# Local attention on array tiles: 64x32 for the scores, 64x64 for P times V

## The reference

```
for layer in range(6):
    h = shift_tokens(x)                      # half of the channels from the token before
    q, k, v = split(h @ Wqkv[layer], 3)      # 16 heads x 64 each
    q, k = l2norm(q) * q_scale, l2norm(k) * k_scale, then rotary tables
    # windows of 32 queries; each sees the keys of its own window and of the one before
    sim = einsum('bhwie,bhwje->bhwij', q, [k_before, k_own]) * 8.0     # 32 x 64 per window
    sim = where(j < i or j > i + 32 or no such key, -max, sim)
    out = einsum('bhwij,bhwje->bhwie', softmax(sim), [v_before, v_own])
    x = out @ Wo[layer] + x
    x = (a * gelu(gate)) @ W2 + b2 + x,   with a, gate = layernorm(shift_tokens(x)) @ W1 + b1
```

## Time and the profile before

| | |
|---|---|
| median of 3 runs | 1647.47 us (1647.35 to 1647.62) |
| profiled execution, its own time | 1648.04 us |
| its span | 1646.3 us |
| PE busy | 1580.4 us (96%) |
| VectorE busy | 1421.3 us (86%) |
| GpSimd busy | 1369.4 us (83%) |
| ScalarE busy | 1331.9 us (81%) |

### The profile page before, as it was taken

One profiled execution on the slowest core, in us unless ns is written; L12 is line 12 of the kernel. 1 busy time (PEld: TensorE's weight loads), 2 busy tenths in 40 slices (PEclk: granted clock), 3 DMA queues, 4 the chain that ended last, 5 costly groups with the idle time before them and its releaser, 6 DMA issues.

```text
span 1646.3 us, 51246 instructions
## 1 busy us (share of the span) xinstructions
PE 1580.4 (96%) x20015; PEld 1345.6 (82%) x20015; DVE 1421.3 (86%) x2163; ACT 1331.9 (81%) x2516; POOL 1369.4 (83%) x1323
## 2 busy tenths in 40 slices
PE   5999999999999999999999999999999999999976
PEld 3778888888888888888888888888888888888865
DVE  7888888989888888888888888889888899999964
ACT  5778788888888888888888888888888888888862
POOL 8888899888899888889888889988889777777632
PEclk9999999999999999999999999999999999999998
DMA  5334222433332334333343232334323222322231
GB/s 146 96 85 130 74 86 76 119 113 89 98 94 67 107 101 115 83 90 91 84 124 103 82 99 73 104 87 129 96 72 101 66 78 71 88 76 66 64 85 28
DMA packets 182430, 149.64 MB, mean 91 GB/s; under 512 B 133804, under 2 KB 153904, under 8 KB 182192
## 3 DMA queue, kind: packets, MB, share of 16 engines
q1 hardware_dynamic: 182192, 146.35, 31.7%
HBM read 27.56 MB, written 1.05 MB: 17 GB/s over the span
## 4 chain that ended last, share of the span: by engine, by line
PE 67%; DVE 12%; issue 6%; ACT 5%; POOL 4%; SPq 2%; DMA 2%; ACTq 0%; DVEq 0%; POOLq 0%
PE ps_pv L851 10%; PE ps_s L827 8%; PE ps_pv L872 7%; PE ps_tr L788 7%; PE ps_qn L763 7%; PE ps_qn L765 5%; PE ps_qn L764 5%; PE ps_tr L775 4%; PE ps_pv L863 3%; DVE ss L1513 3%; DVE v_new L1524 2%; PE ps_qn L910 2%; POOL qk L1967 2%; PE ps_qn L911 2%; PE ps_qn L912 2%
## 5 line engine op out<-in xcount | busy, mean ns | idle before, releaser
L1967 POOL TENSOR_TENSOR qk<-qk,t 128x1024 f32<-128x1024 f32 x192 | 458.9, 2392 | 42.2 <-DVE qk L1503 40.8
L1500 DVE TENSOR_TENSOR t<-ps_qn,tab 128x512 f32<-128x512 f32 x384 | 264.9, 690 | 119.6 <-ACT sq L1150 109.6
L1979 POOL TENSOR_TENSOR qkr<-qk,rinv 128x1024 f32<-128x1024 f32 x192 | 361.5, 1904 | 7.5
L763 PE MATMUL ps_qn<-w_hi,xs_hi 128*128 128x512 f32 x576 | 262.7, 456 | 10.7 <-DVE qk L1503 7.4
L1137 ACT ACTIVATE pbd<-ps_tr 64x512 f32<-64x512 f32 x384 | 226.0, 589 | 45.7 <-PE ps_tr L775 42.5
L1503 DVE TENSOR_TENSOR qk<-ps_qn,tab 128x512 f32<-128x512 f32 x384 | 261.6, 681 | 0.0
L1150 ACT ACTIVATE sq<-ps_qn 128x512 f32<-128x512 f32 x384 | 229.2, 597 | 32.1 <-PE ps_qn L765 27.3
L1182 ACT ACTIVATE qbd<-ps_tr 64x512 f32<-64x512 f32 x384 | 227.9, 593 | 18.9 <-PE ps_tr L788 12.5
L764 PE MATMUL ps_qn<-w_lo,xs_hi 128*128 128x512 f32 x576 | 228.5, 397 | 0.0
L765 PE MATMUL ps_qn<-w_hi,xs_lo 128*128 128x512 f32 x576 | 228.5, 397 | 0.0
L1513 DVE TENSOR_REDUCE ss<-sq 128x32 f32<-128x2048 f32 x96 | 216.7, 2257 | 0.2 <-issue 0.2
(11 more groups left out here) (173 smaller groups left out, 3247.3 us busy)
## 6 DMA issues: line engine op xcount, KB each, us to landing
v_own<-v_new SPq DMA_DIRECT2D x96, 512.0 KB, 3.2
v_back<-v_new SPq DMA_DIRECT2D x96, 384.0 KB, 3.5
v_back<-v_own SPq DMA_DIRECT2D x94, 128.0 KB, 2.4
kT<-kT SPq DMA_DIRECT2D x84, 128.0 KB, 3.4
w_raw<-in_Wqkv SPq DMA_DIRECT2D x18, 512.0 KB, 4.9
rot<-in_rot SPq DMA_DIRECT2D x48, 128.0 KB, 2.6
wo<-in_Wo SPq DMA_DIRECT2D x6, 512.0 KB, 4.5
x<-x SPq DMA_DIRECT2D x48, 56.0 KB
```

The costliest lines, as they stand in the source:

```text
L763: mm(ps_qn[bank][:, :], xs_hi[b][:, :], w_hi[:, part], start=True, stop=False)
L1500: v.tensor_tensor(t2[:, part].rearrange("p (h s d) -> p h s d", s=2, d=DH // 2), swapped, tab[:, 2 * k + 1:2 * k + 2, :].rearrange("p o (s ...
L1967: g.tensor_tensor(qk[b][:, part], qk[b][:, part], t2[:, part], ALU.add).then_inc(added[b], 1)
L1979: g.tensor_tensor(qkr[b][:, part].rearrange("p (h d) -> p h d", d=DH), qk[b][:, part].rearrange("p (h d) -> p h d", d=DH), rinv[b][:, k * ...
```

## The change

Scores and P times V use smaller array tiles whose stationary operands are plain.

- **Scores**: the queries go to `qT` as they are transposed (128 rows x 8 head pairs x 128 tokens). Each matmul holds 32 queries of one head (64 rows x 32 columns) and moves 64 keys; 64 matmuls a half, on eight array tiles (2 row halves x 4 column quarters). `ps_s` is laid out by row half: one bank for each.
- **P times V**: the probabilities go to `pT`, 64 keys on the rows of each half. Each matmul holds 64 keys x 64 columns of the values of a head and moves 32 query columns; 64 matmuls a half, on four array tiles. The two banks of `ps_pv` now belong to the two row halves, and both are full only at the end of f=1.
- **Values**: instead of `v_own` and `v_back` there is `v_win`, for each window its 64 keys on 64 rows, the even heads' on the lower half and the odd heads' on the upper. `move_v` makes it with ten DMAs where there were three.
- **Mask**: two matmuls of 128 rows, no longer of 64.
- **ScalarE**: `evac_probs` and `evac_q` copy 128 rows at once, no longer twice 64.
- **Start and end**: two memsets on GpSimd are gone; in the last steps `scale_probs` of the last half is moved ahead of `low_fxn` and `last_root` there.
- The host permutes columns of `Wqkv` and rows of `Wo` for the new order.

```diff
+V_CARRY, V_MOVE = 2 * 16, 8 * 16
...
-    w.v_own = per_stream("v_own", [P, INNER])
-    w.v_back = per_stream("v_back", [P, INNER])
-    w.qbd = sb("qbd", [P, HP, 4, 2, WINDOW])
+    w.v_win = per_stream("v_win", [P, WINDOWS, HP * DH])
+    w.qT = sb("qT", [P, HP, P])
...
-    w.pbd = sb("pbd", [P, HP, 2, 2, 2, WINDOW])
+    w.pT = sb("pT", [P, HP, P])
...
-        def pv_target(bank, m, h):
-            return ps_pv[bank][DH * h:DH * (h + 1), :].rearrange("p (m u a q) -> p m u a q", m=4, u=2, a=2)[:, m // 2, :, m % 2, :]
+        def pv_rows(bank):
+            return ps_pv[bank][:, :].rearrange("p (g t) -> p g t", g=HP // 2)
...
                 def move_v(i, b):
...
-                    if j.first:
-                        values = a["no_keys"].rearrange("(r k) h w -> r (k h w)", r=WINDOW)
-                    else:
-                        wait_fill(sp, pv_full, pv_order, i, ("pv", b, 1))
-                        values = v_own[b][P - WINDOW:P, :]
-                    sp.dma_start(v_back[b][0:WINDOW, :], values).then_inc(v_carried[b], 16)
+                    def window(h, w, first, last):
+                        return v_win[b][DH * h + first:DH * h + last, w, :]
+
+                    def tokens(h, first, last):
+                        return v_new[b][first:last, h * HP * DH:(h + 1) * HP * DH]
+
+                    if not j.first:
+                        for h in range(2):
+                            wait_fill(sp, pv_full, pv_order, i, ("pv", b, h))
+                    for h in range(2):
+                        if j.first:
+                            values = a["no_keys"].rearrange("(r k) h w -> r (k h w)", r=WINDOW)[:, h * HP * DH:(h + 1) * HP * DH]
+                        else:
+                            values = window(h, WINDOWS - 1, WINDOW, 2 * WINDOW)
+                        sp.dma_start(window(h, 0, 0, WINDOW), values).then_inc(v_carried[b], 16)
                     wait_fill(sp, qn_done, qn_order, j, ("qkv", b, 5))
-                    sp.dma_start(v_back[b][WINDOW:P, :], v_new[b][0:P - WINDOW, :]).then_inc(v_moved[b], 16)
-                    sp.wait_ge(v_carried[b], (j.n + 1) * 16)
-                    sp.dma_start(v_own[b][:, :], v_new[b][:, :]).then_inc(v_moved[b], 16)
+                    for h in range(2):
+                        sp.dma_start(window(h, 0, WINDOW, 2 * WINDOW), tokens(h, 0, WINDOW)).then_inc(v_moved[b], 16)
+                        for w in (1, 2):
+                            sp.dma_start(window(h, w, 0, 2 * WINDOW), tokens(h, WINDOW * (w - 1), WINDOW * (w + 1))).then_inc(v_moved[b], 16)
+                    sp.wait_ge(v_carried[b], (j.n + 1) * V_CARRY)
+                    for h in range(2):
+                        sp.dma_start(window(h, 3, 0, 2 * WINDOW), tokens(h, 2 * WINDOW, P)).then_inc(v_moved[b], 16)
...
                 def mask(i, b):
...
-                    for f in range(2):
-                        rows = slice(64 * f, 64 * f + 64)
-                        mm(ps_s[:, 4 * f:4 * f + 4, :, :].rearrange("p m u k -> p m (u k)"), sel_bf[rows, :],
-                           mask_bf[rows, min(j.tile, 1):min(j.tile, 1) + 1, :].broadcast_to([64, 4, P]), start=True, stop=False)
+                    kind = min(j.tile, 1)
+                    for h in range(2):
+                        mm(ps_s[:, h, :, :].rearrange("p m k -> p (m k)"), sel_bf[:, :],
+                           mask_bf[:, kind:kind + 1, :].broadcast_to([P, HP, 2 * WINDOW]), start=True, stop=False)
...
                 def scores(i, b, f):
...
                     for hp in range(4 * f, 4 * f + 4):
-                        for u in range(2):
-                            for odd in range(2):
-                                w = 2 * u + odd
-                                last = mm(ps_s[64 * odd:64 * odd + 64, hp, u, :],
-                                          qbd[:, hp, w, :, :].rearrange("p h q -> p (h q)"),
-                                          kT[b][:, hp, WINDOW * w:WINDOW * (w + 2)], start=False,
-                                          stop=(hp % 4 == 3 and u == 1))
+                        for h in range(2):
+                            rows = slice(DH * h, DH * (h + 1))
+                            for w in range(WINDOWS):
+                                q = slice(WINDOW * w, WINDOW * (w + 1))
+                                last = mm(ps_s[q, h, hp, :], qT[rows, hp, q], kT[b][rows, hp, WINDOW * w:WINDOW * (w + 2)],
+                                          start=False, stop=hp == HP - 1)
...
                 def probs_v(i, b, f):
...
-                    bank, n = fill(pv_order, i, ("pv", b, f))
-                    ring_free(pe, pv_done, bank, n)
-                    for m in range(8):
-                        hp, odd = 4 * f + m // 2, m % 2
-                        v = (v_own if odd else v_back)[b]
-                        for h in range(2):
-                            head = 2 * hp + h
-                            last = mm(pv_target(bank, m, h), v[:, head * DH:(head + 1) * DH],
-                                      pbd[:, hp, odd, h, :, :].rearrange("p u q -> p (u q)"), start=True, stop=True)
-                    last.then_inc(pv_full[bank], 1)
+                    fills = [fill(pv_order, i, ("pv", b, h)) for h in range(2)]
+                    if f == 0:
+                        for bank, n in fills:
+                            ring_free(pe, pv_done, bank, n)
+                    for g in (2 * f, 2 * f + 1):
+                        for h, (bank, _) in enumerate(fills):
+                            rows = slice(DH * h, DH * (h + 1))
+                            for w in range(WINDOWS):
+                                q = slice(WINDOW * w, WINDOW * (w + 1))
+                                for c in range(2):
+                                    hp = 2 * g + c
+                                    last = mm(pv_rows(bank)[DH * c:DH * (c + 1), g, q], v_win[b][rows, w, hp * DH:(hp + 1) * DH],
+                                              pT[rows, hp, q], start=True, stop=True)
+                            if g == HP // 2 - 1:
+                                last.then_inc(pv_full[bank], 1)
...
-                    wait_fill(act, pv_full, pv_order, pi, ("pv", pb, k))
+                    for h in range(2):
+                        wait_fill(act, pv_full, pv_order, pi, ("pv", pb, h))
                     bank, n = fill(tr_order, i, ("probs", b, k))
                     act.wait_ge(tr_full[bank], n)
-                    for u in range(2):
-                        rows = slice(DH * u, DH * (u + 1))
-                        last = f(pbd[rows, 4 * k:4 * k + 4, :, :, u, :].rearrange("p m a h q -> p (m a h) q"),
-                                 ps_tr[bank][rows, :].rearrange("p (x q) -> p x q", q=WINDOW), ACT.Copy)
-                    last.then_inc(tr_done[bank], 1)
+                    f(pT[:, 4 * k:4 * k + 4, :].rearrange("p m t -> p (m t)"), ps_tr[bank][:, :], ACT.Copy).then_inc(tr_done[bank], 1)
...
-                    for h in range(2):
-                        rows = slice(DH * h, DH * (h + 1))
-                        last = f(qbd[rows, 4 * k:4 * k + 4, :, h, :],
-                                 ps_tr[bank][rows, :].rearrange("p (m w q) -> p m w q", m=4, w=4), ACT.Copy)
-                    last.then_inc(tr_done[bank], 1)
+                    f(qT[:, 4 * k:4 * k + 4, :].rearrange("p m t -> p (m t)"), ps_tr[bank][:, :], ACT.Copy).then_inc(tr_done[bank], 1)
...
-                    g.memset(qbd[:, :, :, :, :], 0.0)
-                    g.memset(pbd[:, :, :, :, :, :], 0.0)
...
                     scale_probs(Step(0, STEPS - 2), 1)
                     scale_probs(Step(0, STEPS - 1), 0)
+                    scale_probs(Step(0, STEPS - 1), 1)
                     low_fxn(END + 1)
                     last_root(END + 1)
-                    scale_probs(Step(0, STEPS - 1), 1)
```

More of the change, by code:

```diff
@@ L26 @@
 HP = HEADS // 2
+WINDOWS = P // WINDOW
 FF = int(DIM * 4 * 2 / 3)
@@ L870, in project_out @@
                         wait_fill(pe, pv_done, pv_order, i, ("pv", b, f))
-                    for hp in range(HP):
-                        last = mm(ps_pv[bank][:, 0:P], oT[:, hp, :, :, :].rearrange("p u a q -> p (u a q)"), wo[:, hp, :],
-                                  start=(hp == 0), stop=(hp == HP - 1))
+                    for n in range(HP):
+                        last = mm(ps_pv[bank][:, 0:P], oT[:, n // 2, n % 2, :], wo[:, n, :], start=(n == 0), stop=(n == HP - 1))
                     return last
@@ L2196, in mask_constants @@
 def mask_constants():
-    m = np.full((2, 2, WINDOW, 2, 2, 2 * WINDOW), MASKED, np.float32)
+    m = np.full((WINDOWS, WINDOW, 2, 2 * WINDOW), MASKED, np.float32)
     q = np.arange(WINDOW)[:, None]
@@ L2202, in mask_constants @@
     ok = (k >= q) & (k <= q + WINDOW)
[L2203 to L2212 removed]
+    for w in range(WINDOWS):
+        for kind in range(2):
+            seen = ok & ((k >= WINDOW) if (w, kind) == (0, 0) else True)
```

(2 more changed lines are left out.)

49 lines of the change are left out of this document (21 added, 28 removed).

## The result

The changed kernel takes 1800.06 us (median of 4 runs, 1786.21 to 1816.87) against 1647.41 for the kernel before (4 runs). The slowest of the four counts as slow and stays out of the ratio, which is 1.090 with a 95% interval of 1.081 to 1.099; the median of the other three is 1790.78. The change cost 152 us by the medians of all runs, and 143 by the median of the three. The forecast was 1672, 25 us slower, so that the loss was about six times the forecast one and the time far outside of the range of 1628 to 1706. The sign was right and the size was not.

What follows compares the result with a forecast made beforehand. PE, busy 96%, was taken as full but in balance with a loop through VectorE and ScalarE. From 1648.0, value moves +33 −4 +3, drain −6 and start −1 gave 1673, or 1672 against the median; range 1628 to 1706.

Steps and rivals of the forecast that it cites:

- The loop, and PE's saved work as no gain: VectorE's less_max, PE's mask and burst two, squares, back to less_max: PE's saved 0.8 us bring 0 in b=0, −0.35 in b=1.
- I take 0.62 from start to start: SyncE's queue: the ten value transfers of a half are issued 0.62 us apart, whatever their size.
- 8.0 us: First value carry to last landing: 9×0.62=5.6 plus 2.4; evac_v in b=0 then misses 1.1, taken as +33 over 33 halves.
- In b=1 ... −0.1 for 37 halves: VectorE's evac_v in b=1: 0.4 us missing, less 0.35 of the loop and lateness of b=0, so −4 in all.
- I take 1.08 unchanged: A burst of P times V on PE: 64 passes on four tiles, 16 each, still take 1.08 us.
- rival B: PE's tiles don't overlap across row halves: a burst of P times V 2.16, scores 2.0, whole 1870 us; chance 0.04.
- Scores 1.0 us: Scores on PE: 128 passes on eight tiles, 16 on each, take 1.0 us, −1.0 us a half.
- C: PE passes can't follow closer than 31.5 and 34 ns on any tiles: scores 4.0, burst 2.2, whole 2060 us; chance 0.03.
- Mask 0.5, and squares later behind both evacuations: PE's mask of two 128-row products takes about 0.5, +0.2; both evac_pv wait for burst two, so squares start +0.3 later.
- ScalarE at nothing: ScalarE's evacuations of probabilities and queries take 2.4 us less a half, costed at nothing in the total.
- Drain −6: End of the kernel: earlier scale_probs on GpSimd saves 4.2 us and fewer copies about 2, together −6.
- Start −1: Before the first tile's scores: the queries' copies shrink from 2.42 to 1.2 us, taken as −1.

Runs made afterwards that it cites:

- three_moves_wide_pv: Changed kernel with three value transfers instead of ten and P times V back on 128x64 stationary pieces (output wrong): 1640.20 us, ratio 0.995 to the kernel before.
- before_ten_moves: Kernel before with only its three value transfers a half split into ten of the same bytes: 1715.23 us, ratio 1.040.
- wide_scores_interleaved_pv: Changed kernel with three value transfers, scores on 128x64 pieces and row halves innermost in P times V (output wrong): 1659.46 us, ratio 1.007 to the kernel before.
- before_drain: Kernel before with only the last half's scale_probs moved ahead of low_fxn and last_root on GpSimd: 1643.34 us, ratio 0.996.
- tile_scores: Kernel before with plain queries in qT and scores in 64 matmuls on 64x32 tiles, in the old layout of the scores: 1660.72 us, ratio 1.008.
- after_three_moves: Changed kernel with three value transfers a half instead of ten, same bytes, values in wrong places: 1717.08 us, ratio 1.042 to the kernel before.
- before_seven_tiny: Kernel before with seven 16-byte transfers added between its second and third value transfers in SyncE's queue: 1764.35 us, ratio 1.070.

## Why the prediction was wrong

The mechanism that carried the forecast was the right one: ten issues hold back VectorE. Three steps failed. The loss in b=1 was put at nothing, the burst of P times V was left at its length, and neither the supply of instructions nor the clock had a term. So the sum had +25 us where 143 to 152 came.

- **The loop, and PE's saved work as no gain** (right as far as tested). The one kernel with short scores that is below the kernel before, three_moves_wide_pv, owes 6 of its 8 us to the drain.
- **"I take 0.62 from start to start", "8.0 us"** (right for the issues, 0.64, and in b=1 of the step above for the landing, 2.33). In b=0 the last landing took 3.66, not 2.4, and `evac_v` began 9.50 after the first carry, which is 2.6 more than the 6.86 of before, not 1.1. There VectorE waited 31 times, 56 us, where 33 times one us were forecast.
- **"In b=1 ... −0.1 for 37 halves"** (wrong, the first large step). VectorE waited 32 times there, 50 us, 1.22 of them in the step above. The row that the forecast used, 813.86, shows VectorE idle for 0.59 before it; part of the 50 us takes the place of such idleness, as the 23.5 us above that fell to 4.2. Undoing the issues gave back 83 us of the changed kernel (before_ten_moves: 67 from the other side), where the sum had +33 −4 +3=32.
- **"I take 1.08 unchanged"** for a burst of P times V (wrong, the second large step). It took 1.41. The text bounded it by 0.54 and 2.16 (rival B) and took a value at which the row halves overlap fully. In the order of this change they do so only in part; alternating, the burst was busy for 1.14 where it had been for 1.46. Two bursts of 0.33 in 94 halves are 62 us; the order alone gave 44 back in wide_scores_interleaved_pv.
- **Scores 1.0 us** (wrong, and worse than idle). They took 1.48 busy, and the 128 additional instructions a half in them brought stops. The forecast had no term for instruction supply; the rivals B and C asked how fast passes can follow each other, never whether they arrive. On the first question the runs are clear: 128 passes in about 1.4 us are 11 ns each, and C falls; the floor of about 25 ns that the Trainium skill gives in "TensorE: Matmul & The Clock Gate", "Wait — 56ns, not 53.3ns?", isn't seen for passes on different tiles. With P times V on its tiles, wide scores were 13 us faster.
- **The clock** (left out). Idle microseconds such as those before 607 were followed by a stretch at 1.2 GHz, and there were 93 us at that level against 16. If PE set the end all through them, the 77 more cost 38. It is probably less: two executions of the kernel before took 1649.04 and 1649.06 us with mean clocks of 0.997 and 0.988. No run separates the clock from the stops that bring it.
- **Mask 0.5, and squares later behind both evacuations** (right for the mask, 0.54). The second is consistent with the 1.76 and 1.61 us that VectorE stood idle before L1510's third product in the step above (0.99 in the earlier trace rows), but most of that belongs to the bursts: with the old burst length and the late evacuations the wait of the whole span was 118.0 against 109.6.
- **ScalarE at nothing** (right): 251 us less work, and three_moves_wide_pv, which has it too, is within 2 us of before_drain's gain.
- **Drain −6** (right: 6.0 in before_drain, 6.7 on top of tile_scores). **Start −1** was not tested.

Together: the 83 and the 68 of after_three_moves add up to the whole because they part it in two. The independent number is the 67 of before_ten_moves: 67 for the issues and 68 for the rest of the change (with the drain's −6 in it) are 135 of the 143 to 152. The two are not independent, as the stops of either bring the lower clock for both.

## What to carry to other kernels

Count the instructions of a finer tiling before its work: each DMA costs its queue the same however small, and a group of 64 short fp32 matmuls, 256 instructions with their passes and weight loads, can outrun the supply of instructions. When array tiles are to run side by side, let neighbouring matmuls alternate between all of them, and see that the output's layout uses them all. In a kernel whose engines are tied in one loop, ask what stands between the last issue and the waiting engine, for that slack (here 0.9 us) is used up long before any engine is full.

## What the runs showed of the hardware

- SyncE needed 0.62 us to issue a 16-byte transfer, 0.56 to 0.61 for 64 to 128 KB of values and 0.52 for 512 KB (L600 of before_seven_tiny).
- Tiles in different row halves overlapped better when neighbours in the stream: 64 passes on 64x64 tiles took 1.46 us in blocks of a row half and 1.14 alternating. The scores on eight 64x32 tiles took 1.48 in both orders, and 1.99 on four.
- PE stopped for 1 to 3.5 us with no semaphore to wait for, at places that repeat with a shift of 256 instructions. PE's instructions come in transfers of 16 KB (163 before, 258 in the changed kernel), and 27 of 29 stops of over 0.7 us in two traces ended 2.2 to 2.7 us after one had started.
- After 3.23 us in which PE was idle, the granted clock was 0.57 of 2.4 GHz in the next nine microseconds of full work.
